# The bias copy of the middle score bank, moved one exponential back, in a two-layer graph kernel

## The reference, cut to what matters

```python
q = (x @ Wq.T).reshape(d, n, h)        # d = 128 heads, n = 3327, h = 8
k = (x @ Wk.T).reshape(d, n, h)
v = (x @ Wv.T).reshape(d, n, h)
a = jnp.einsum('dnh,dmh->dnm', q, k) * scale
a = a + spatial_encoding + edge_encoding   # both are adj
a = jax.nn.softmax(a, axis=2)
out = jnp.einsum('dnm,dmh->dnh', a, v)
return out.reshape(n, h * d) @ Wo.T
```

## Time and profile before

| | |
|---|---|
| Median of 3 runs | 14255.69 us (14249.31 to 14256.35) |
| The profiled execution's own time | 14252.36 us |
| its span, first to last instruction | 14250.2 us |
| mean granted TensorE clock | 0.991; 1.00 from 1000 us to 14000 us |
| busy share of the span: PE / DVE / ACT / POOL | 96% / 94% / 94% / 2% |
| exponentials, bias copies, sweeps | 26624, 3328, 13312 |

### The profile page before, as it was taken

One profiled execution on the slowest core, in us unless ns is written; L12 is line 12 of the kernel. 1 busy time (PEld: TensorE's weight loads), 2 busy tenths in 40 slices (PEclk: granted clock), 3 DMA queues, 4 the chain that ended last, 5 costly groups with the idle time before them and its releaser, 6 DMA issues. The chain is left out here.

```text
span 14250.2 us, 392441 instructions
## 1 busy us (share of the span) xinstructions
PE 13631.5 (96%) x145131; PEld 4628.5 (32%) x145131; DVE 13402.4 (94%) x27589; ACT 13391.9 (94%) x30466; POOL 328.2 (2%) x945
## 2 busy tenths in 40 slices
PE   3889999999999999999999999999999999999999
PEld 2533333333333333333333333333333333333334
DVE  4579999999999999999999999999999999999993
ACT  1269999999999999999999999999999999999997
POOL 1100000000000000000000000000000000000000
PEclk7989999999999999999999999999999999999999
DMA  8975655656565565656556565655656565565653
GB/s 277 261 164 138 145 137 136 145 137 145 137 144 138 135 146 137 144 138 143 138 134 147 137 145 136 146 137 135 145 137 144 137 145 136 137 145 136 145 136 97
DMA packets 2075064, 2081.72 MB, mean 146 GB/s; under 512 B 818905, under 2 KB 1827808, under 8 KB 2066752
## 3 DMA queue, kind: packets, MB, share of 16 engines
q1 hardware_dynamic: 2069118, 2043.41, 59.6%
q10 hardware_dynamic: 4032, 13.31, 0.2%
HBM read 1922.23 MB, written 133.76 MB: 144 GB/s over the span
## 5 line engine op out<-in xcount | busy, mean ns | idle before, releaser
L235 DVE CUSTOM_DVE_ANT_0 swept<-X,adj_row 128x832 f32<-128x832 f32 x13312 | 12987.6, 1022 | 269.3 <-PE X L257 50.8
L1006 ACT ACTIVATE prob<-S 128x416 f32<-128x416 f32 x26624 | 11832.6, 518 | 107.1 <-PE S L1074 37.0
L1074 PE MATMUL S<-q_blk,k_res 52*128 52x416 f16 x26624 | 6860.6, 343 | 32.4 <-ACT S L997 14.4
L1095 PE MATMUL O<-prob,v_pad 128*32 128x208 f32 (+1 forms) x88752 | 6741.5, 385 | 2.5
L257 PE MATMUL X<-mk,mq 40*128 40x416 f16 x26624 | 6392.3, 343 | 248.1 <-DVE m_part L235 225.8
L1074 PEld LDWEIGHTS S<-q_blk,k_res 52*128 52x128 f16 x26624 | 2064.8, 93 | 4543.5 <-ACT S L997 1482.7
L1095 PEld LDWEIGHTS O<-prob,v_pad 128*32 128x32 f32 x88752 | 1860.4, 108 | 2509.3 <-issue 2048.1
L257 PEld LDWEIGHTS X<-mk,mq 40*128 40x128 f16 x26624 | 1471.1, 93 | 2121.5 <-DVE m_part L235 1175.7
L997 ACT ACTIVATE S<-adj_key 128x416 f32<-128x416 f32 x3328 | 1751.6, 526 | 35.0
L235 DVE DVE_READ_ACCUMULATOR2_ANT m_part<- 128x1 f32 x13312 | 1107.6, 83 | 0.0
L207 POOL TENSOR_SCALAR m_neg<-m_full 128x16 f32<-128x16 f32 x208 | 52.8, 254 | 12820.3 <-DVE m_full L218 12820.1
(11 more groups left out here) (86 smaller groups left out, 1043.9 us busy)
## 6 DMA issues: line engine op xcount, KB each, us to landing
adj_key<-adj_by_key SPq DMA_DIRECT2D x3328, 208.0 KB, 3.4
adj_row<-in_adj SPq DMA_DIRECT2D x1200, 416.0 KB, 3.8
mk<-k_planes SPq DMA_DIRECT2D x1664, 104.0 KB
adj_row<-adj_tail SPq DMA_DIRECT2D x400, 416.0 KB, 3.9
mk<-k_planes SPq DMA_DIRECT2D x1664, 52.0 KB
row<-in_adj SPq DMA_DIRECT2D x47, 1663.5 KB, 8.1
adj_by_key<-aT SPq DMA_DIRECT2D x26, 1664.0 KB, 11.7
q_planes<-q_parts SPq DMA_DIRECT2D x26, 1024.0 KB, 14.9
```

Of the source, the lines that this page charges most:

```text
L235: nc.vector.tensor_tensor_reduce(out=swept[u % 2][:], in0=x_, in1=adj_row[gi % 4][:].rearrange("p (a b) -> p a b", a=2), scale=1.0, scalar ...
L1006: nc.scalar.activation(prob[c % QR][:, d % 4, :], S[b][:, 0:WB], ACT.Exp, scale=2.0).then_inc(s_e[b], 1)
L1074: nc.tensor.matmul(S[b][:, 0:WB], k_res[base:base + KR, d // 2, s * P:(s + 1) * P], q_blk[n % 2][base:base + KR, d // 2, :], start=False, ...
L1095: done = nc.tensor.matmul(O[32 * d:32 * d + 32, cols], v_pad[:, s, 4 * q + d, :], prob[born(j, q) % QR][:, d, cols], start=first, stop=Tru ...
```

## The change

`LATER` says for each bank whether the bias copy of the next job stands directly behind the last exponential of this one (0) or one exponential later (1). The middle value goes from 0 to 1.

```diff
     HELD = 14
     FIRST = 24
-    LATER = (1, 0, 1)
+    LATER = (1, 1, 1)
     AK = 12
```

## The result

The changed kernel takes 14341.65 us (median of 4 runs, 14339.51 to 14345.37), beside 14252.5 us for the kernel before in the same comparison. The ratio is 1.0063 (95% interval 1.0045 to 1.008): 89 us slower. The profiled execution took 14342.96 us, its span is 14340.7 us, 90.5 us more than before.

The account below looks back on a forecast made before the run. The prediction took the PE and ACT loop of score, exponential and next score as the bound. 1108 x 0.075 = 83 us on 14252.4 gives 14335, and 3.3 more for a median 14338 us; range 14297 to 14364.

Parts of the forecast that it names:

- the ring of PE and ACT: Attention stage: score, exponential, next score of that bank, with value and maxima products between on PE, sets the pace.
- the gain of 0.14 us at each turn: On ACT, the later copy no longer waits for its exponential's full end; taken as 0, 155 us if ACT were pace.
- The loss on PE: Bank 1's first score waits for the later copy: 1.37 us from score 8 to 10, not 1.30; 0.075 us taken.
- chain: Waits from score at 8 through exponential and copy to score at 10: 0.80 + 0.52 + 0.05 = 1.37 us.
- cover: PE's own work from the score at 8 to that at 10, 1.30 us, or 1.29 one cycle earlier.
- Does it come back?: Step asking whether later work absorbs the delay; claimed everything behind moves along, so 0.075 us is paid once a cycle.
- place 10: The first score of bank 1 in a cycle on PE, the one that the change touches.
- ScalarE as the pace: Rival: ACT bounds the kernel, so 0.14 us a turn is gained, 14101 us; chance 0.05.
- Absorption: Rival: a later PE wait ends at the same time as today; fully 14256 us, half 14297; chance 0.09.
- Growth: Rival: TensorE's late start makes a second wait, as at banks 2 and 0; 0.15 us a cycle, 14422 us; chance 0.04.
- what would show it: Signs in the profile after: score 8 to 10 takes 1.37 us, copy-wait idle near nothing, cycle 11.97 us, not 11.89.

Follow-up runs that it names:

- half copy: Bank 1's bias copy writes only 208 of 416 columns: 14255.01 us with the order of the kernel before, 14253.62 us with that of the changed kernel.

## Why the prediction was right

*Where the bound is.* The forecast took the ring of PE and ACT as the pace and not ScalarE's 99% of busy time. The half copy in the order of before bears it out: 0.17 us less work on ScalarE a cycle, no change. So the gain of 0.14 us at each turn was real (the copy starts 0.11 before the end ahead of it, and not 0.04 after) and worth nothing, as its step said. One figure of this step was too large: 27 times 0.40 us leaves out that a copy takes a step of 0.44 and that the direct one costs 0.14 more. With these ScalarE needs 24 x 0.40 + 3 x 0.44 + 0.14 = 11.06 us, so its room in the cycle of 11.89 was 0.83 us and not 1.1. Nothing in the sum rests on it.

*The loss on PE.* It was carried over from bank 2: 0.80 + 0.52 + 0.05 = 1.37. Measured in the cycle shown: copy 8228.05 - 8227.25 = 0.80 after the score at 8, 0.52 long, 0.05 to the score, 1.37. Over all cycles it is 0.802 + 0.516 + 0.059 = 1.377, and bank 2, from which it was taken, had 0.797 + 0.516 + 0.062 = 1.375. The two halves of the comparison, chain and cover, were moved one at a time: the chain shorter (half copy) and the loss went; the chain longer by one exponential and the loss grew by that; the cover longer and the loss went.

*The size.* 0.075 us a turn was taken, and 0.080 came: 83 us forecast for 89. The means over all cycles, 1.377 against 1.296, make it 0.081; two cycles read to 0.01 us could not give that.

*Does it come back?* It was said that all behind place 10 moves along. The distances behind it are the same, 1.37 us from 18 to 20, and from 20 to the next 8 too (7886.49 - 7880.85 = 5.64 before; 8227.25 less 8221.61, the score at 20 one cycle earlier, is 5.64 after; the mean is 5.685 in both). So nothing came back. VectorE's starts did not stay on their own: it idles more.

```profile
8221.61 0.35 PE L1074 MATMUL S<-q_blk,k_res 52*128 52x416 f16 x1
```

*The rivals.* ScalarE as the pace fell with the half copy, and again with bank 2's direct copy. Absorption fell with the steps above. Growth fell: banks 2 and 0, without slack of their own, did not fall behind further. One point of what would show it, that exponentials at 9 and 10 part, holds as well: that at 9 starts at 8228.49, and the row here ends at 8229.52, so that the one at 10, some 0.52 long, starts at 8229.00, 0.51 later and not 0.40.

```profile
8228.49 1.03 ACT L1006 ACTIVATE prob<-S 128x416 f32<-128x416 f32 x2
```

*What was less sharp.* For bank 0 the expectation spanned 0.05 to 0.16 us, and 0.15 came. The trace has the wait that it named: with the direct copy the score at 1 starts 0.056 us after the end of the exponential at 22 on the mean, where it had started 0.478 after it, and from the score at 20 to it the mean went from 2.206 to 2.363 us. So the upper end, 0.16, is what was paid there; where the 0.05 of the lower end would have come from, no run shows.

## What to carry to other kernels

When two engines hand work to each other in a ring, ask at each hand-over which way is longer, the chain through the other engine or this engine's own work between the two ends, and read both from starts of instructions. A wait costs only what the chain is longer than the cover, and a step of 0.4 us was worth 0.08 the first time and 0.41 the second. The same move is right for one bank and wrong for another, since each stands before another piece of cover, so decide place by place, and take the price from a place in the same trace that already has the new order.

## What the runs showed of the hardware

- A copy of 128 x 208 fp32 from SBUF to PSUM on ScalarE was 0.34 us long and one of 128 x 416 was 0.52.
- From the end of a ScalarE instruction to the start of the score that waited for it there were 0.055 to 0.062 us on the mean, for an exponential and for a bias copy alike; from the start of a score to the start of the exponential that waited for it 0.38 to 0.39 (places 10 and 18).
- Busy time on ScalarE grew by 94.9 us with the same instructions while it waited more. The exponential at 9 is 0.51 us long on the mean in both kernels, but the one at 10 starts 0.52 after it where it had started 0.41 after it: the wait took away overlap, and hardly any idle time shows (64.1 us ahead of the exponentials from 2000 to 14000 us before, 88.5 after). The longer wait with the copy two late does show, as 0.44 us.
